# One score buffer for both heads, one exponential over 2048 columns, and two buffers for the gate and up products

## What is computed

```python
xn = layernorm(x)
q, k, v = (split_heads(holo_linear(xn, ...)) for ...)        # 16 heads of 64
attn = softmax(einsum('bhqd,bhkd->bhqk', q, k) * 64 ** -0.5)
att = holo_linear(merge_heads(einsum('bhqk,bhkd->bhqd', attn, v)), ...)
# holo_linear(x) = (x @ basis.T) @ (amp * cos(phase)).T, rank 32
g = silu(einsum('td,edf->etf', xn, w_gate)) * einsum('td,edf->etf', xn, w_up)
y = einsum('te,etd->td', combine, einsum('etf,efd->etd', g, w_down))  # 8 experts, top 2
out = x + att + y + (silu(xn @ sw_gate) * (xn @ sw_up)) @ sw_down     # 8 x 1408 + 2816 hidden
```

## Time and profile before

| what | value |
|---|---|
| median of 3 runs | 4033.52 us (4030.92 to 4036.6) |
| the profiled execution, its own time | 4028.81 us |
| its span on the slowest core (core 7) | 4027.3 us |
| spans of the 8 cores | 4020.2 to 4027.3 us |
| mean granted TensorE clock, cores 0 to 7 | 0.904 to 0.906 |
| PE busy | 3211.3 us, 80% of the span |
| VectorE (DVE) busy | 1823.0 us, 45% |
| ScalarE (ACT) busy | 937.1 us, 23% |

### The profile page before, as it was taken

The page is one execution under the profiler, slowest core; times in us unless marked ns, Lnnn a source line. Parts: engine busy times, 40 slices in busy tenths (PEclk is TensorE's granted clock), DMA queues, the critical chain, the costliest instruction groups (busy, mean ns, idle before and its releaser), DMA issues.

```text
span 4027.3 us, 46942 instructions; the slowest of 8 cores (4020.2 to 4027.3 us)
## 1 busy us (share of the span) xinstructions
PE 3211.3 (80%) x13795; PEld 1236.1 (31%) x13795; DVE 1823.0 (45%) x2660; ACT 937.1 (23%) x1201; POOL 267.5 (7%) x351
## 2 busy tenths in 40 slices
PE   2444366666666469999999999999999999999996
PEld 1111011111111124333343443333434344344432
DVE  4444543334443334455444444545444445443344
ACT  0222266666666101000111111000111111011100
POOL 1000000000000010000110000000100000011000
PEclk9755588988888679999999999999999999999995
DMA  1000000000000063333344333333434333334205
GB/s 33 26 25 15 0 1 1 1 1 1 1 1 1 11 63 32 32 32 32 35 48 44 32 32 32 32 32 32 44 38 45 32 32 32 32 32 49 31 1 157
DMA packets 254444, 116.11 MB, mean 29 GB/s; under 512 B 233592, under 2 KB 233592, under 8 KB 254208
## 3 DMA queue, kind: packets, MB, share of 16 engines
q0 software_dynamic: 245248, 87.87, 21.0%
q1 hardware_dynamic: 8960, 25.24, 2.1%
HBM read 191.40 MB, written 8.39 MB: 50 GB/s over the span
## 4 chain that ended last, share of the span: by engine, by line
PE 68%; ACT 13%; DVE 9%; issue 7%; DMA 2%; DVEq 1%; POOL 0%; ACTq 0%; SPq 0%; POOLq 0%
PE p_xg L830 19%; PE p_xu L839 19%; PE p_d L872 19%; ACT pTs L653 6%; ACT pTs L646 6%; PE p_stB L638 3%; PE p_t L411 2%; DVE acc L880 1%; PE p_a L608 1%; PE p_b L608 1%; PE p_stA L627 1%; DMA out<-o 1%; PE p_pj L295 1%; DVE gbuf L854 1%; DMA wdbuf<-w_down 1%
## 5 line engine op out<-in xcount | busy, mean ns | idle before, releaser
L872 PE MATMUL p_d<-gbuf,wdbuf 128*128 128x512 bf16 x3520 | 835.9, 378 | 64.8 <-DVE acc L880 35.1
L830 PE MATMUL p_xg<-xnh_fm,wgbuf 128*128 128x512 bf16 x3520 | 844.3, 383 | 26.8 <-DMA wdbuf<-w_down 26.8
L839 PE MATMUL p_xu<-xnh_fm,wubuf 128*128 128x512 bf16 x3520 | 835.3, 380 | 0.0
L849 ACT ACTIVATE sgt<-p_xg 128x512 bf16<-128x512 f32 x440 | 262.7, 597 | 2178.4 <-PE p_xg L830 1577.0
L854 DVE TENSOR_TENSOR gbuf<-sgt,p_xu 128x512 bf16<-128x512 bf16 x440 | 302.5, 688 | 981.1 <-PE p_xu L839 981.1
L880 DVE TENSOR_TENSOR acc<-acc,p_d 128x512 f32<-128x512 f32 x896 | 617.2, 689 | 258.9 <-PE p_d L872 243.0
L830 PEld LDWEIGHTS p_xg<-xnh_fm,wgbuf 128*128 128x128 bf16 x3520 | 346.5, 99 | 451.0 <-issue 43.3
L839 PEld LDWEIGHTS p_xu<-xnh_fm,wubuf 128*128 128x128 bf16 x3520 | 345.8, 98 | 420.0 <-issue 8.5
L872 PEld LDWEIGHTS p_d<-gbuf,wdbuf 128*128 128x128 bf16 x3520 | 285.1, 96 | 611.0 <-issue 391.7
L638 PE MATMUL p_stB<-q_fm,k_fm 64*128 64x512 bf16 x512 | 176.6, 429 | 252.4 <-ACT pTs L653 251.8
L646 ACT ACTIVATE pTs<-p_stA,bias 128x1024 bf16<-128x1024 f32 x256 | 285.3, 1114 | 279.0 <-PE p_stA L627 234.9
(11 more groups left out here) (203 smaller groups left out, 1189.2 us busy)
## 6 DMA issues: line engine op xcount, KB each, us to landing
wgbuf<-w_gate POOLq DMA_DIRECT2D x88, 256.0 KB, 13.9
wubuf<-w_up POOLq DMA_DIRECT2D x88, 256.0 KB, 15.1
wdbuf<-w_down POOLq DMA_DIRECT2D x88, 256.0 KB, 15.9
x_tm<-x SPq DMA_DIRECT2D x16, 512.0 KB, 3.9
x<-x SPq DMA_DIRECT2D x16, 512.0 KB, 4.6
out<-o SPq DMA_DIRECT2D x16, 512.0 KB, 5.3
wgbuf<-sw_gate POOLq DMA_DIRECT2D x22, 256.0 KB, 10.9
wubuf<-sw_up POOLq DMA_DIRECT2D x22, 256.0 KB, 11.4
```

The source lines that it names most:

```text
L830: emit("tensor", lambda te, buf=buf, loc=loc, c=c, tg=tg: te.matmul(p_xg[:, :], wgbuf[buf][:, loc * 1024 + c * 128: loc * 1024 + c * 128 + ...
L839: emit("tensor", lambda te, buf=buf, loc=loc, c=c, tg=tg: te.matmul(p_xu[:, :], wubuf[buf][:, loc * 1024 + c * 128: loc * 1024 + c * 128 + ...
L849: emit("scalar", lambda s, ss=ss: s.activation(sgt[ss][:], p_xg[:, :], AF.Silu), waits=[("t", t_xg), sgt_free[ss]], incs=[("s", 1)])
L872: first=(li == 0), last=(li == len(grp) - 1): te.matmul(pb[:, :], wdbuf[buf][:, li * 1024 + dc * 128: li * 1024 + dc * 128 + 128], gbuf[bu ...
```

## The change

Three edits. (a) In attention `p_stA` and `p_stB` become one buffer `p_st` of four banks, which holds one step of both heads. The four score matmuls of a step wait together for the exponential of the step before, and one exponential of 2048 columns takes the place of two of 1024. `p_c`, a bank of its own, takes `p_stB`'s place in L731. (b) In the expert part `p_xg` and `p_xu` get two banks each, used in turn. (c) The waits follow. No matmul, no VectorE instruction and no DMA is added or taken away; 256 ACTIVATE instructions go.

```diff
-    p_stA = pt("p_stA", [128, 2048], F32, stx)
-    p_stB = pt("p_stB", [128, 1024], F32, stx)
+    p_st = pt("p_st", [128, 2048], F32, stx)
...
-                            waits=([("s", exp_done[sidx][p2])] if j == 0 else []) +
+                            waits=([("s", exp_done[p2])] if (sidx == 0 and j == 0) else []) +
...
-                    pTs_free[(sidx, pp2)] = ("t", cnt["t"])
+                pTs_free[pp2] = ("t", cnt["t"])
...
+                first = True
                 for j in (0, 1):
...
+                    for sidx, h in ((0, hA), (1, hB)):
...
+                             sidx=sidx, j=j: te.matmul(
+                                 p_st[:, sidx * 1024 + j * 512: sidx * 1024 + j * 512 + 512],
...
+                            waits=(st_free if first else []) +
...
+                        first = False
+                t_sp = cnt["t"]
                 emit("scalar", lambda s, pp=pp: s.activation(
-                    pTs[:, pp * 2048: pp * 2048 + 1024],
-                    p_stA[:, pp * 1024: pp * 1024 + 1024], AF.Exp,
+                    pTs[:, pp * 2048: pp * 2048 + 2048],
+                    p_st[:, 0:2048], AF.Exp,
                     scale=0.125, bias=bias128[:]),
...
-                    waits=[("t", t_spB), pTs_free[(1, pp)]], incs=[("s", 1)])
-                st_freeB = [("s", cnt["s"])]
-                exp_done[1][pair] = cnt["s"]
+                    waits=[("t", t_sp), pTs_free[pp]], incs=[("s", 1)])
+                st_free = [("s", cnt["s"])]
+                exp_done[pair] = cnt["s"]
...
-            pbank = p_b[:, :] if slot == 0 else p_stB[:, 0:512]
+            pbank = p_b if slot == 0 else p_c
...
-    p_xg = pt("p_xg", [128, 512], F32, st3p)
-    p_xu = pt("p_xu", [128, 512], F32, st3p)
+    p_xg = [pt(f"p_xg{b}", [128, 512], F32, st3p) for b in range(2)]
+    p_xu = [pt(f"p_xu{b}", [128, 512], F32, st3p) for b in range(2)]
...
+                gb = xgu_slot[0]
+                xgu_slot[0] ^= 1
+                pg_b = p_xg[gb]
+                pu_b = p_xu[gb]
...
-                        waits=([dww, pxg_free] if c == 0 else []),
+                        waits=([dww, pxg_free[gb]] if c == 0 else []),
...
-                        waits=([pxu_free] if c == 0 else []),
+                        waits=([pxu_free[gb]] if c == 0 else []),
```

More of the change, by code:

```diff
@@ L539, in build_nc @@
     p_b = pt("p_b", [128, 512], F32, st2p)
+    p_c = pt("p_c", [128, 512], F32, st2p)
     pa_free = [("v", v_p1_done), ("s", s_p1_done)]
@@ L589, in build_nc @@
     rrow_free = [("dr0", 0), ("dr1", 0)]
-    st_freeA = {0: [("s", s_p1_done), ("v", v_p1_done)],
-                1: [("s", s_p1_done), ("v", v_p1_done)]}
-    st_freeB = [("s", s_p1_done), ("v", v_p1_done)]
+    st_free = [("s", s_p1_done), ("v", v_p1_done)]
     av_free = {0: list(pa_free), 1: list(pbc_free[0])}
-    pTs_free = {(si, pp): ("t", 0) for si in (0, 1) for pp in (0, 1)}
+    pTs_free = {0: ("t", 0), 1: ("t", 0)}
     pairs = [(2 * hp, 2 * hp + 1, qb) for hp in range(NHEAD // 2) for qb in range(NTG)]
     for mi, (hA, hB, qb) in enumerate(pairs):
-        exp_done = {0: [0] * 8, 1: [0] * 8}
+        exp_done = [0] * 8
         for pair in range(10):
@@ L617, in build_nc @@
                             incs=[("t", 1)])
-                    pTs_free[(sidx, pp2)] = ("t", cnt["t"])
+                pTs_free[pp2] = ("t", cnt["t"])
             if pair < 8:
                 pp = pair % 2
-                c8A, offA = hA // 2, (hA % 2) * 64
-                c8B, offB = hB // 2, (hB % 2) * 64
-                t_spA = t_spB = 0
+                first = True
                 for j in (0, 1):
[L625 to L645, removed]
@@ new lines, in build_nc @@
+                    for sidx, h in ((0, hA), (1, hB)):
+                        c8, off = h // 2, (h % 2) * 64
+                        kc = 2 * pair + j
+                        emit("tensor", lambda te, c8=c8, off=off, kc=kc, qb=qb,
+                             sidx=sidx, j=j: te.matmul(
+                                 p_st[:, sidx * 1024 + j * 512: sidx * 1024 + j * 512 + 512],
+                                 k_fm[off:off + 64, c8 * T + kc * 128: c8 * T + kc * 128 + 128],
+                                 q_fm[off:off + 64, c8 * T + qb * 512: c8 * T + qb * 512 + 512],
+                                 start=True, stop=True),
+                            waits=(st_free if first else []) +
+                                  ([("v", v_bias)] if (mi == 0 and pair == 0 and first)
+                                   else []),
+                            incs=[("t", 1)])
+                        first = False
@@ L646, in build_nc @@
+                t_sp = cnt["t"]
                 emit("scalar", lambda s, pp=pp: s.activation(
-                    pTs[:, pp * 2048: pp * 2048 + 1024],
-                    p_stA[:, pp * 1024: pp * 1024 + 1024], AF.Exp,
+                    pTs[:, pp * 2048: pp * 2048 + 2048],
+                    p_st[:, 0:2048], AF.Exp,
                     scale=0.125, bias=bias128[:]),
-                    waits=[("t", t_spA), pTs_free[(0, pp)]], incs=[("s", 1)])
-                st_freeA[pp] = [("s", cnt["s"])]
@@ L710, in build_nc @@
     pa_free2 = [av_free[0][0]]
-    pbc_free2 = {0: [("v", v_onorm)] + list(av_free[1]),
-                 1: [("v", v_onorm)] + list(st_freeB)}
+    pbc_free2 = {0: ("v", v_onorm), 1: ("v", v_onorm)}
     for tg in range(NTG):
@@ L729, in build_nc @@
             slot = (c8 * NTG + tg) % 2
-            pbank = p_b[:, :] if slot == 0 else p_stB[:, 0:512]
+            pbank = p_b if slot == 0 else p_c
             emit("tensor", lambda te, c8=c8, tg=tg, pb=pbank: te.matmul(
-                pb, wT["o"][:, c8 * 128:(c8 + 1) * 128],
+                pb[:, :], wT["o"][:, c8 * 128:(c8 + 1) * 128],
                 res_bf[:, tg * 512: tg * 512 + 512], start=True, stop=True),
-                waits=[("s", s_reso)] + pbc_free2[slot], incs=[("t", 1)])
+                waits=[("s", s_reso), pbc_free2[slot]], incs=[("t", 1)])
             t_ao = cnt["t"]
             emit("vector", lambda v, c8=c8, tg=tg, pb=pbank: v.tensor_copy(
-                acc[:, c8 * T + tg * 512: c8 * T + tg * 512 + 512], pb),
+                acc[:, c8 * T + tg * 512: c8 * T + tg * 512 + 512], pb[:, :]),
                 waits=[("t", t_ao)], incs=[("v", 1)])
-            pbc_free2[slot] = [("v", cnt["v"])]
+            pbc_free2[slot] = ("v", cnt["v"])
     v_acc0 = cnt["v"]
@@ L796, in build_nc @@
     grp_last_t = [0] * len(groups)
-    pxg_free = ("v", v_acc0)
-    pxu_free = ("v", v_acc0)
+    pxg_free = [("v", v_acc0), ("v", v_acc0)]
+    pxu_free = [("v", v_acc0), ("v", v_acc0)]
+    xgu_slot = [0]
     pd_free = {0: ("v", v_acc0), 1: ("v", v_acc0)}
@@ L828, in build_nc @@
             for tg in range(NTG):
+                gb = xgu_slot[0]
+                xgu_slot[0] ^= 1
+                pg_b = p_xg[gb]
+                pu_b = p_xu[gb]
                 for c in range(NC8):
-                    emit("tensor", lambda te, buf=buf, loc=loc, c=c, tg=tg: te.matmul(
-                        p_xg[:, :],
+                    emit("tensor", lambda te, buf=buf, loc=loc, c=c, tg=tg, pb=pg_b: te.matmul(
+                        pb[:, :],
                         wgbuf[buf][:, loc * 1024 + c * 128: loc * 1024 + c * 128 + 128],
@@ L838, in build_nc @@
                 for c in range(NC8):
-                    emit("tensor", lambda te, buf=buf, loc=loc, c=c, tg=tg: te.matmul(
-                        p_xu[:, :],
+                    emit("tensor", lambda te, buf=buf, loc=loc, c=c, tg=tg, pb=pu_b: te.matmul(
+                        pb[:, :],
                         wubuf[buf][:, loc * 1024 + c * 128: loc * 1024 + c * 128 + 128],
@@ L848, in build_nc @@
                 su_slot += 1
-                emit("scalar", lambda s, ss=ss: s.activation(sgt[ss][:], p_xg[:, :], AF.Silu),
+                emit("scalar", lambda s, ss=ss, pb=pg_b: s.activation(sgt[ss][:], pb[:, :], AF.Silu),
                      waits=[("t", t_xg), sgt_free[ss]], incs=[("s", 1)])
-                pxg_free = ("s", cnt["s"])
+                pxg_free[gb] = ("s", cnt["s"])
                 s_silu = cnt["s"]
                 gslice = gbuf[buf][:, loc * T + tg * 512: loc * T + tg * 512 + 512]
-                emit("vector", lambda v, gs=gslice, ss=ss: v.tensor_tensor(
-                    gs, sgt[ss][:], p_xu[:, :], ALU.mult),
+                emit("vector", lambda v, gs=gslice, ss=ss, pb=pu_b: v.tensor_tensor(
+                    gs, sgt[ss][:], pb[:, :], ALU.mult),
                     waits=[("t", t_xu), ("s", s_silu)] +
@@ L858, in build_nc @@
                     incs=[("v", 1)])
-                pxu_free = ("v", cnt["v"])
+                pxu_free[gb] = ("v", cnt["v"])
                 sgt_free[ss] = ("v", cnt["v"])
```

## The result

| | before | after |
|---|---|---|
| median | 4034.47 us (10 runs) | 3965.82 us (9 runs) |
| ratio, with 95% interval | | 0.985 (0.9822 to 0.9879) |
| the same pair on another chip | 4030.37 us | 3961.78 us, 0.9833 (0.9818 to 0.9849) |
| there, mean over the cores in place of the slowest core | 4023.6 us | 3957.6 us |
| attention, first exponential's start to the last one's end | 841.2 us on most cores, 840.6 to 842.3 | 776.5 us (two cores 774.7) |

The forecast was 3963 us, 71 under before; the change gave 69, of which the profiles find 64.7 in attention.

A forecast was written before the change was run, and what follows sets the result against it. TensorE bounds the experts' stage; in attention no engine is full and a loop of waits sets each step. Attention -71 us, other edits 0: 4033.5 - 71 = 3962.5, predicted 3963 us, 8-in-10 range 3942 to 4010.

The forecast's parts named there:

- One ACTIVATE of 2048 columns: Attention: one exponential of 2048 columns takes 1.965 us, extrapolated from copies of 128 and 512 columns.
- Rival B: Attention: the wide exponential costs what its two halves cost, 2.15 to 2.23 us; 4010 to 4031 us; chance 0.06.
- The gap: Attention at the high clock: from one exponential's end to the next one's start, 0.90 us instead of 0.70.
- At the low clock: Attention at 1.2 GHz: 1.32 us between exponentials, a step of 3.285 us instead of 3.34.
- The turn: Attention, passage from one block to the next: 3.845 us against 4.00, 31 times, -4.8 us in all.
- 0.6 us of cover: Attention, start of a block: VectorE frees `p_b` 0.6 us before the next L608 needs it, so no wait.
- Low steps: Attention steps at 1.2 GHz: 16 remain where 64 were, one in every second block, each 0.42 us dearer.
- Sum: Attention in total: -66.1 us from steps within blocks, -4.8 from block changes, last block's end within 0.5; -71 us.
- ordinary steps: Attention, the 224 steps within blocks: 224 x 2.865 + 16 x 0.42 = 648.5 us against 714.6, -66.1.
- Rival A: Attention: the clock stays low throughout, if the grant follows the array's streaming time; +57 us, 4091 us; chance 0.12.
- Rival C: Expert stage: two banks let TensorE run ahead through remaining waits, so it gains too; 3945 us; chance 0.03.

## Why the prediction was right

- **One ACTIVATE of 2048 columns**: 1.965 forecast, 1.967 measured. The extrapolation from two widths of another function held. The Trainium skill's 280 + 0.833 ns a column (ScalarE: Activation LUTs, "What ACT_TABLE_LOAD costs") gives 1986, 1% over; the trace has 1967. Rival B falls.
- **The gap**: 0.90 forecast from the turn, 0.92 measured, 5 us over 224 steps. **At the low clock** 1.32 and 1.34.
- **The turn**: 3.845 forecast, 3.86 measured. But nothing was won against the turn before. The prediction set 3.845 against a mean of 4.00 and did not ask why its own rows add up to 2 x 1.11 + 0.20 + 1.42 = 3.85. Of the 31 turns before, 16 took 3.86 and 15 took 4.14, with an exponential that came 0.28 late in them (last section). The 4.8 us booked here came out as 4.1 because these late ones left the turns: right by luck. VectorE's copies cost nothing there, as said; 0.6 us of cover was the estimate. With the blocks joined that cover was gone, and the wait of 0.48 appeared.
- **Low steps**: 16 taken, about 14 measured. The reason held: fewer of the denser turns make the clock fall, 9 of 31 where before nearly all did, and with neither turn nor held matmul there is no fall. The nearness of 14 to 16 is partly luck, for it was to be one low step in every second block and came as 9 falls of one or two. Incomplete was the view that only a turn can do it: two matmuls held back by 0.48 us did it as well. No run gives a rule with a number.
- **Sum**: ordinary steps 648.5 forecast; the starts of the exponentials add up to 655.0 (714.8 before, 714.6 forecast), turns 119.5 (119.2). The missing 6.5 us are the gap's 0.02 a step and eight delays of 0.28 (last section), less two low steps. So the gain in attention is 64.7 us, 6 short of the forecast. The medians give 68.7 because they follow the slowest core, and the other stages differ by a few us from core to core in either kernel; the mean over the cores fell by 66.0 us. That 69 came so near to 71 is partly luck.
- **Rival A** had the right sign for a kernel whose step gets longer: with two exponentials the clock fell to 0.83. Its mechanism fell with the run without B's scores. The Trainium skill's picture (TensorE: Matmul & The Clock Gate, "A second HAM failure mode: psum-queue depth-cycling") of banks cycled with short idle pieces does not fit the traces here: the kernel with three score buffers in turn waits for a free one 249 times, up to 0.9 us, and its clock does not fall once the first block is under way.
- **Rival C**: no gain from the second banks, shown by either edit alone.

## What to carry to other kernels

Before a double buffer is given up or added, write down the loop of waits that sets a step: here one wide ACTIVATE saved 0.46 us and the lost overlap cost 0.22, and in the expert part a second bank met no wait at all. Then ask whether the loop can go altogether: three smaller buffers in turn kept ScalarE running and gained more than twice as much as the change. Where the clock falls at a regular place, look for a gap between loops and for a matmul that comes late there, even one that delays nothing by itself. Before a term is set against a mean, see whether the mean hides two values.

## What the runs showed of the hardware that was not expected

- In these runs the grant did not go by the time that PE was busy: with head B's score matmuls left out, fewer rows in use and the same busy pattern, it was 0.52 instead of 0.97.
- A matmul of 64 rows can start ahead of one queued before it when its own half of the array is free, as far as the starts tell: four in the order A, A, B, B took 0.61 us like four in A, B, A, B, and two of them started within 0.03 us.
- Every 32nd ACTIVATE of attention comes 0.28 us late. Before, that fell on every second block (turns of 4.14 against 3.86, 15 of 31); after, with half as many instructions, on every fourth (8 waits of 1.20 instead of 0.92, the 9.6 us in the waits above). The cause was not tried; it is worth 2.2 us of the gain.
